# A short TensorE form for the last group of an expert in a mixture-of-experts stage

## The reference, cut to what matters

```python
y = jnp.einsum('eci,eih->ech', jax.nn.silu(g) * u, w_down)   # g, u: einsum('ech,ehi->eci', xg, w_gate / w_up)
out = jnp.zeros((T + 1, H), x.dtype).at[t_slot].add(w_slot[:, None] * y)
```

## Time and profile before

| | |
|---|---|
| median of 3 runs | 2299.56 us (2298.75 to 2300.44) |
| profiled execution, first to last instruction (span) | 2155.5 us |
| median less span | 144.1 us |
| TensorE, share of the span | 1944.1 us busy (90%) |
| VectorE / ScalarE / GpSimd | 73% / 56% / 73% |
| the experts' block | about 1096 us to 2155 us of the span |
| mean DMA rate between 1100 us and the end | 170 GB/s |

### The profile page before, as it was taken

How to read it: one execution, slowest core, us unless ns; L and a number is a source line. 1 busy time by engine, 2 the same in 40 slices (tenths; PEclk the granted TensorE clock), 3 DMA queues, 4 the chain that set the end, 5 groups by cost and what they waited for, 6 DMA issues and landing times. The chain is left out here.

```text
span 2155.5 us, 66447 instructions
## 1 busy us (share of the span) xinstructions
PE 1944.1 (90%) x22263; PEld 1463.4 (68%) x22296; DVE 1582.7 (73%) x3230; ACT 1203.0 (56%) x3018; POOL 1575.2 (73%) x1776
## 2 busy tenths in 40 slices
PE   0799999999999999997259999999999999999997
PEld 0677667777667766675146777777777777777775
DVE  5688888888888888985236676777766667767664
ACT  3466666666666666665135555555554555545553
POOL 6336778777777777876667777777767777777775
PEclk9999999999999999999579999999999999999999
DMA  3111110111101111101048888777788888887876
GB/s 108 38 34 37 40 39 30 34 34 40 39 29 34 34 39 39 32 27 43 16 111 172 186 193 160 176 181 171 167 178 186 170 178 182 169 190 156 184 153 103
DMA packets 141452, 222.72 MB, mean 103 GB/s; under 512 B 32944, under 2 KB 65840, under 8 KB 141360
## 3 DMA queue, kind: packets, MB, share of 16 engines
q0 software_dynamic: 74752, 144.02, 33.9%
q1 hardware_dynamic: 62000, 69.24, 10.4%
q10 hardware_dynamic: 4608, 8.39, 1.0%
HBM read 136.34 MB, written 96.73 MB: 108 GB/s over the span
## 5 line engine op out<-in xcount | busy, mean ns | idle before, releaser
L2162 POOL DMA_INDIRECT out_dram<-y,m_add x300 | 498.1, 1660 | 171.0 <-POOLq L2170 112.5
L2288 PE MATMUL ps<-xh,wh 128*128 128x256 f16 x1752 | 398.3, 273 | 4.7 <-PEq L2300 4.7
L2289 PE MATMUL ps<-xh,wl 128*128 128x256 f16 x1752 | 398.3, 273 | 0.0
L2154 POOL DMA_INDIRECT xg<-z_scratch,slot_t x292 | 295.8, 1013 | 96.4 <-issue 83.4
L630 POOL DMA_INDIRECT slot_scratch<-pair,slots x256 | 304.8, 1191 | 70.2 <-issue 58.1
L2365 ACT ACTIVATE y<-ps,wts_now 128x512 f32<-128x512 f32 x294 | 185.2, 681 | 143.4 <-ACTq L2364 143.4
L2293 PE MATMUL ps<-xl,wh 128*128 128x256 f16 x1752 | 239.0, 273 | 1.3 <-PEq L2304 1.3
L2439 DVE SCALAR_TENSOR_TENSOR hx<-ps,s 64x256 f16<-64x256 f32 x146 | 62.2, 426 | 216.3 <-DVEq L2462 215.6
L2381 ACT ACTIVATE xh<-ps 128x512 f16<-128x512 f32 x146 | 87.2, 597 | 224.0 <-ACTq L2380 224.0
L2288 PEld LDWEIGHTS ps<-xh,wh 128*128 128x128 f16 x1752 | 171.3, 98 | 45.9 <-issue 12.8
L2289 PEld LDWEIGHTS ps<-xh,wl 128*128 128x128 f16 x1752 | 171.4, 98 | 33.1
(11 more groups left out here) (345 smaller groups left out, 5001.4 us busy)
## 6 DMA issues: line engine op xcount, KB each, us to landing
wst<-in_L_ffn_w_gate_dram SPq DMA_DIRECT2D x32, 384.0 KB
wst<-in_L_ffn_w_up_dram SPq DMA_DIRECT2D x32, 384.0 KB
xt<-in_x_dram SPq DMA_DIRECT2D x32, 256.0 KB
ct<-in_ctx_dram SPq DMA_DIRECT2D x32, 256.0 KB, 2.6
out_dram<-x SPq DMA_DIRECT2D x32, 256.0 KB, 2.1
z_scratch<-zn ACTq DMA_DIRECT2D x32, 256.0 KB, 2.0
wdst<-in_L_ffn_w_down_dram SPq DMA_DIRECT2D x32, 256.0 KB
out_dram<-y,m_add POOLq DMA_INDIRECT x300, 5.1
```

The lines of the kernel that those rows point to most:

```text
L2154: pool.indirect_dma_start(out=xg[b][:, h, :], out_offset=None, in_=z_d[:, :], in_offset=bass.IndirectOffsetOnAxis(ap=rows(h), axis=0)).the ...
L2162: pool.indirect_dma_start(out=acc_d[:, :], out_offset=bass.IndirectOffsetOnAxis(ap=m_add[:, k, h:h + 1], axis=0), in_=y[:, k, h, :], in_of ...
L2288: pe.matmul(ps[:, dst, 0:GROUP], wh[:, j, k, c0:c0 + P], xh[:, k, :], start=(k == 0), stop=False)
L2289: pe.matmul(ps[:, dst, 0:GROUP], wl[:, j, k, c0:c0 + P], xh[:, k, :], start=False, stop=False)
```

## The change

TensorE gets a short form of a group for a last group of at most 128 rows. `turn(b, 1)` turns only the first half (4 transposes). `gate_up(j, P)` streams 128 columns instead of 256. The short group's `down`, which is issued with the following group, computes only the first half (5 matmuls of 512 columns) and one matmul of 8 columns that stands in for the second half so that `y_ps` still comes twice. A register `few` carries to the next expert whether the last group was short. To choose, TensorE tests `n > g * GROUP + P` in each written-out group and in the small loop, with a full body and a short body, and tests `few` ahead of each expert's first group, again with two bodies (`first(1)` and `first(2)`). The other engines do the same work as before, on 256 rows; where a short form wrote nothing, they process what an earlier group left. On GpSimd one test becomes the `Else` of the test before it.

```diff
                     if more:
                         with pool.If(n <= 4 * GROUP):
                             gather_group(e + 1, 1, 1)
-                        with pool.If(n > 4 * GROUP):
+                        with pool.Else():
                             gather_group(e + 1, 0, 0)
...
-                def turn(b):
+                def turn(b, halves=2):
...
-                            for h in range(2):
+                            for h in range(halves):
...
-                def down(j, b=None):
+                def down(j, b=None, halves=2):
...
+                    if halves == 1:
+                        pe.matmul(ps[:, 6, 0:8], hl1[:, P:2 * P], dh[:, j, 0, 0:8], start=True, stop=True).then_inc(y_ps, 1)
-                def gate_up(j):
+                def gate_up(j, cols=GROUP):
...
                 def expert(e, j, more):
-                    turn(0)
-                    down(1 - j, 0)
-                    pe.wait_ge(wh_ready[j], 1)
-                    pe.sem_inc(wh_ready[j], -1)
+
+                    def first(halves_before):
+                        turn(0)
+                        down(1 - j, 0, halves_before)
+                        pe.wait_ge(wh_ready[j], 1)
+                        pe.sem_inc(wh_ready[j], -1)
+                        gate_up(j)
+
+                    with pe.If(pe.snap(few, min_val=0, max_val=1) > 0):
+                        first(1)
+                    with pe.Else():
+                        first(2)
+                    turn(1)
+                    down(j, 1)
                     gate_up(j)
+                    n = count_of(pe, e)
+                    pe.reg_mov(few, 0)

                     def group(g, b):
-                        turn(b)
-                        down(j, b)
-                        gate_up(j)
-                    group(1, 1)
-                    n = count_of(pe, e)
+                        with pe.If(n > g * GROUP + P):
+                            turn(b)
+                            down(j, b)
+                            gate_up(j)
+                        with pe.Else():
+                            turn(b, 1)
+                            down(j, b)
+                            gate_up(j, P)
+                            pe.reg_mov(few, 1)
                     written_out_groups(pe, n, group)
...
                 pairs_of_experts(pe, expert)
-                down(1)
+                with pe.If(pe.snap(few, min_val=0, max_val=1) > 0):
+                    down(1, halves=1)
+                with pe.Else():
+                    down(1)
```

More of the change, by code:

```diff
@@ L2249, in _ @@
                     pe.reg_mov(n_landed[b], 0)
-                def turn(b):
+                few = pe.alloc_register("few")
+                pe.reg_mov(few, 0)
+                def turn(b, halves=2):
                     pe.reg_add(n_landed[b], n_landed[b], 32)
@@ L2279, in down @@
                     pe.sem_inc(hl1_ready, -1)
-                    for h in range(2):
+                    for h in range(halves):
                         o, t = ps[:, 5 + h, :], slice(h * P, h * P + P)
                         pe.matmul(o, hl1[:, t], dh[:, j, 0, :], start=False, stop=True).then_inc(y_ps, 1)
-                def gate_up(j):
+                    if halves == 1:
+                        pe.matmul(ps[:, 6, 0:8], hl1[:, P:2 * P], dh[:, j, 0, 0:8], start=True, stop=True).then_inc(y_ps, 1)
+                def gate_up(j, cols=GROUP):
                     def with_xh(c0, dst):
                         for k in range(KC):
-                            pe.matmul(ps[:, dst, 0:GROUP], wh[:, j, k, c0:c0 + P], xh[:, k, :], start=(k == 0), stop=False)
-                            pe.matmul(ps[:, dst, 0:GROUP], wl[:, j, k, c0:c0 + P], xh[:, k, :], start=False, stop=False)
+                            pe.matmul(ps[:, dst, 0:cols], wh[:, j, k, c0:c0 + P], xh[:, k, 0:cols], start=(k == 0), stop=False)
+                            pe.matmul(ps[:, dst, 0:cols], wl[:, j, k, c0:c0 + P], xh[:, k, 0:cols], start=False, stop=False)
                     def with_xl(c0, dst, signal):
                         for k in range(KC):
-                            m = pe.matmul(ps[:, dst, 0:GROUP], wh[:, j, k, c0:c0 + P], xl[:, k, :], start=False,
+                            m = pe.matmul(ps[:, dst, 0:cols], wh[:, j, k, c0:c0 + P], xl[:, k, 0:cols], start=False,
                                           stop=(k == KC - 1))
```

## The result

| | before | after |
|---|---|---|
| median | 2299.64 us (2298.75 to 2300.44, 4 runs) | 2530.28 us (2523.12 to 2532.47, 4 runs) |
| ratio | | 1.1001, 95% interval 1.0985 to 1.1017 |

The change makes the kernel 230.6 us slower. The forecast was 2440 us (its sum: 144 us slower), with a range of 2340 to 2580: the sign, the mechanism and the range held, and the sum fell short by 87 us.

What follows compares the result with a forecast made beforehand. TensorE, busy 90% of the span, was taken to set the pace. Expert ends 60, back edges 29 and short jumps 55 sum to 144 us on top of 2299.6: about 2444, stated as 2440 us, range 2340 to 2580.

Steps and rivals of the forecast that it cites:

- back edges: Start of the pair loop fetched again: 59 us if the hint does not help, 0 if it does; half taken, 29.
- short jumps: 113 jumps over some 110 instructions at groups' bodies; 48 leave the packet, half wait 2.3 us: 55 us, bounds 0 to 127.
- The loop no longer stays in the engine: TensorE's loop over expert pairs, 189 KB, exceeds what stays resident; 11.6 packets per pair, fetched anew each iteration; chance 0.84.
- Rival 1: TensorE's new loop stays resident and each branch costs 0.22 us: 2284 us (2278 to 2292), chance 0.12.
- Expert ends, 60: Last jumps at 31 expert ends: 32 us for 12 after full groups, 28 for 19 after short ones, 16 us gain included.
- Straight code hides a fetch: On TensorE, fetches in straight code cost nothing; branches to absent code took 4.23 and 3.67 us, against 0.22 when present.
- The clock: After a 3 us wait, granted clock 0.60 loses 1.3 us; some 25 long waits add 30, in the upper bound 2576.
- The short form, 16 us at 19 ends: Gain at short last groups: 1.05 us at 10 ends, 0.7 at 8 pair ends, of TensorE's 3.36; 16 us in all.
- Rival 2: TensorE's whole saving in short groups arrives, 64 us: 2236 us, chance 0.01.
- The time outside the span: 144.1 us of the measured time lie outside the profiled span of 2155.5 us, the same before and after.

Runs made afterwards that it cites:

- Experiment 1: Kernel before plus one, two or four never-run group bodies per expert on TensorE (118, 132, 161 KB loops): 1.0070, 1.0894, 1.0959 of before.
- experiment 5: Kernel before with short transposes and gate/up, full down, in group 4: 0.9980; in 3 and 4, group 5 in small loop: 0.9981; that move alone: 1.0019.
- experiment 4: Kernel after with transposes and down full, only 128-column gate/up kept: 1.1461 on the faster chip; 1.1290 beside all bodies full (1.1330) and the kernel after (1.0985).
- all bodies full: Kernel after with its short bodies made full, all tests and branches kept, 3079 instructions: 2615.11 us, 1.1354; run again 2604.82 us, 1.1330.

## Why the prediction was right, and where its size came short

The sum, against the kernel before on the same kind of chip: the two spans differ by 221.1 us (2521.4 and 2300.3). Of these, 0.7 lie ahead of the experts' block, 10.3 behind the start of the last group, and 210.2 between the first transpose of the block and that of the last group (1278.5 us in the profile after, 1068.3 before). It splits by kind of group (each period runs to the next group's first transpose):

| groups | before | after | difference | forecast |
|---|---|---|---|---|
| last, full, 12 | 90.1 | 202.2 | 112.1 | 32 |
| last, short, 18 | 126.2 | 183.0 | 56.8 | 28, with the first group after |
| back edges | in the two rows above | | | 29 |
| first groups of experts 1 to 31 | 225.8 | 262.9 | 37.1 | part of the 55; clock in the bounds |
| groups 1 to 4 in the middle | 587.8 | 588.7 | 0.9 | 55, short jumps |
| expert 0 | 38.4 | 41.6 | 3.2 | 0 |

- **The loop no longer stays in the engine: right.** Experiment 1 shows it with nothing else changed. Rival 1 (it stays) is refuted; a gain of its kind, 4 us, is seen only in experiment 5, where the loop fits. 171 packets in 1196 us, at 81.2 us for a pair (TensorE's 15 tests at L2111 lie from 1292.8 to 2429.2 us), are 11.6 for each, the forecast.
- **Expert ends, 60: the step that failed most.** I gave each of the 31 ends one wait of 2.5 us. An expert of three or four groups jumps several times in a row: past the two bodies of each group that it doesn't run, then past the rare ones, then to the next expert's code, and each target has to be fetched. I had counted jumps past the untaken half of a group that runs and left out the jumps past groups that don't. At the end of expert 4 three branches took 3.04, 3.65 and 3.36 us one behind the other. A full last group took 16.9 us on average (202.2 / 12) instead of 7.5. With the 51 us of the back edges taken off, the two kinds of last group rose by 118 us, where 60 were in the sum. Besides, one such branch takes 4.5 us in the median and not 3.9.
- **Short jumps, 55: about 10 in the middle groups.** 24 branches at L2127, L2335 and L2324 waited (71 us of branch time), 14 of them at expert ends. Ten of the 80 middle groups have a wait at L2335, of 1.7 to 3.3 us. They took 79.5 us, 9.9 more than 10 x 6.96. The view of L2335 around one of them and TensorE's next transposes:

```profile
L2335 PEldq COMPARE_BRANCH  x3: 68/68/2062, 1351.7 to 1359.9; - x3
```
```profile
1360.17 1.09 PE L2262 MATMUL ps<-ident,xg 128*128 128x128 f32 x8 [0.40 <-issue]
```

So a wait of 2.06 us left TensorE idle for 0.40: the matmuls queued in front of it, 1.95 us in the prediction's working, cover most of it. The table's 0.9 us hides these 10 us, because the late silu of the slower chip cost the other 70 groups 21.8 us and the 80 of the kernel before 30.9. Experiment 4 on the faster chip doesn't test this term: with its code no branch at L2335 took over 0.42 us.

- **Straight code hides a fetch: right inside a group, wrong behind a jump.** The middle groups show the first. Behind a jump that seems to land near a packet's end, a second fetch followed at once, 3.46 us in experiment 4. The working had one fetch for a jump.
- **The clock: in the bounds, and it belonged in the sum.** I had put 1.3 us for each of some 25 long waits into the upper bound alone. The granted clock behind the waits was 0.50, the mean 0.912 against 0.960 in the kernel before on that chip, and the first groups, which run behind the waits, took 37.1 us more, 1.2 each. How much of that is the clock was not separated.
- **The short form, 16 us at 19 ends: right in its mechanism and nearly in size where the code fits** (0.96 and 0.61 against 1.05 and 0.7). In the kernel after it was worth more, some 36 us by the split of experiment 4, so here the sum was off the other way. Rival 2, the whole of TensorE's 64 us, is refuted where the code fits, and where it doesn't as well: half of `down` arrived whole (1.30 us against 1.02), but 128 columns gave 6 us of 36.
- **The time outside the span: wrong,** and without effect on the difference. The profile shown and the times shown were of chips of different speed.

So the total is nearer than its terms, and that is luck: expert ends (58), back edges (22), first groups (37) and what lies behind the start of the last group (10) came out some 127 us above the sum, the short jumps 45 below it.

Still open: why the silu is late in some groups on the slower chip, and in which, why the packet starts later when the branch is reached sooner, and whether the second wait in experiment 4 is due to placement, which was inferred and not tested by moving the code.

## What to carry to other kernels

Count the instructions of a loop on each engine before adding a second form of its body: beyond what stays resident a taken jump to code that has to be fetched took 1.7 to 6.2 us here, mostly 3 to 5, even where the added code never runs. This short form takes 3.4 us from TensorE. Count every jump on the path, those past groups that don't run above all, and the back edge. Below the limit the short form is worth what the next engine in the chain lets through, here two fifths of TensorE's saving or less; and times from different chips are compared only as ratios to the same kernel.

## What the runs showed of the hardware that was not expected

- The step is sharp: 118 KB of loop 1.007, 132 KB 1.089, 161 KB 1.096 of the time before.
- Three chips ran the same program at 2159, 2298 and 2304 us, each within 0.3% of its own median. Between the two profiles, 114 of the 145 us are in the first block, where the granted clock differs (34.1 against 29.7 us an iteration, 0.95 against 1.00 from 300 to 500 us), and the rest in the experts' block, where ScalarE's silu starts up to 1.2 us late with no mark on TensorE's own records. No run shows the cause of either.
- The same operations at another place in the code waited a second time: 12 first groups with all bodies full, 43 us in sum, and none of them with 96 instructions fewer of 3079, by what looks like placement.
